# Attention: projection and row maxima in one block, four heads a unit, and q turned once

## The reference, cut to what matters

```python
qkv = x @ w_attn.T;  q, k, v = split(qkv, 3)      # 32 heads of 16
q, k = rope(q), rope(k)
scores = q @ k.T / 4;  scores[above the diagonal] = -inf
y = softmax(scores) @ v
ak, av = split(adapter_wte @ w_attn.T, 3)[1:]     # 10 rows
y = y + gating * softmax(q @ ak.T / sqrt(512)) @ av
out = y @ w_proj.T
```

## Time and profile before

| what | value |
|---|---|
| median of 3 runs | 2019.07 us (2018.42 to 2019.97) |
| the profiled execution's own time | 2018.18 us |
| its span | 2016.4 us |
| granted TensorE clock, mean | 0.954 of full |
| TensorE matmul, weight load busy | 1873.7 us (93%), 1486.5 us (74%) |
| VectorE, ScalarE, POOL busy | 1386.6, 1172.4, 1367.8 us |

### The profile page before, as it was taken

One profiled execution on the slowest core, in us unless ns is written; L12 is line 12 of the kernel. 1 busy time (PEld: TensorE's weight loads), 2 busy tenths in 40 slices (PEclk: granted clock), 3 DMA queues, 4 the chain that ended last, 5 costly groups with the idle time before them and its releaser, 6 DMA issues. The chain is left out here.

```text
span 2016.4 us, 32469 instructions
## 1 busy us (share of the span) xinstructions
PE 1873.7 (93%) x10700; PEld 1486.5 (74%) x10700; DVE 1386.6 (69%) x1799; ACT 1172.4 (58%) x2109; POOL 1367.8 (68%) x1349
## 2 busy tenths in 40 slices
PE   6989998766999999999999999999999999999967
PEld 4855776555788778777878787787788788877855
DVE  5547454567676787678778767876787687668756
ACT  3221333334776667576757766675767577667723
POOL 4000100352999799789969996997899699969844
PEclk9966899877999999999999999999999999999978
DMA  3000000103334233233333432332333334323301
GB/s 105 1 1 11 12 1 1 32 27 100 115 124 122 82 108 115 86 115 121 105 97 100 132 109 92 99 122 80 117 120 112 90 109 127 105 95 97 118 19 56
DMA packets 174859, 170.35 MB, mean 84 GB/s; under 512 B 11072, under 2 KB 142272, under 8 KB 174656
## 3 DMA queue, kind: packets, MB, share of 16 engines
q1 hardware_dynamic: 173696, 167.84, 27.2%
q10 hardware_dynamic: 960, 0.05, 0.0%
HBM read 165.22 MB, written 2.62 MB: 83 GB/s over the span
## 5 line engine op out<-in xcount | busy, mean ns | idle before, releaser
L143 PE MATMUL ps<-mix_xnT_hi,mix_w_hi 128*128 128x512 f32 x1152 | 463.8, 403 | 12.1 <-DVE mix_xT L1529 6.3
L145 PE MATMUL ps<-mix_xnT_hi,mix_w_lo 128*128 128x512 f32 x1152 | 455.9, 396 | 0.0
L144 PE MATMUL ps<-mix_xnT_lo,mix_w_hi 128*128 128x512 f32 x1152 | 455.5, 395 | 0.0
L1529 DVE SCALAR_TENSOR_TENSOR mix_xT<-ps,mix_cur,mix_xT 128x510 f32<-128x510 f32 x378 | 279.2, 745 | 140.1 <-ACT mix_xT L1396 131.2
L1347 POOL TENSOR_SCALAR_AFFINE_SELECT mix_spread<-mix_spread 128x256 f32<-128x256 f32 x512 | 308.1, 636 | 0.0
L1549 DVE TENSOR_TENSOR mix_decay<-mix_decay,mix_cb 128x1536 f32<-128x1536 f32 x128 | 302.7, 2402 | 4.5 <-ACT mix_decay L1422 4.5
L143 PEld LDWEIGHTS ps<-mix_xnT_hi,mix_w_hi 128*128 128x128 f32 x1152 | 217.9, 189 | 68.1 <-issue 12.5
L1445 ACT ACTIVATE mix_g_hi<-mix_gated 128x512 fp32r<-128x512 f32 x128 | 81.0, 633 | 318.2 <-POOL mix_gated L1324 286.2
L1420 ACT ACTIVATE mix_decay<-mix_spread,mix_cur_ncum 128x256 f32<-128x256 f32 x512 | 253.7, 495 | 13.2 <-DVE mix_cur_ncum L1601 13.2
L145 PEld LDWEIGHTS ps<-mix_xnT_hi,mix_w_lo 128*128 128x128 f32 x1152 | 217.6, 189 | 51.1
L144 PEld LDWEIGHTS ps<-mix_xnT_lo,mix_w_hi 128*128 128x128 f32 x1152 | 218.1, 189 | 47.3
(11 more groups left out here) (262 smaller groups left out, 3409.7 us busy)
## 6 DMA issues: line engine op xcount, KB each, us to landing
mix_spread<-cum_rows SPq DMA_DIRECT2D x128, 512.0 KB, 3.8
mix_w_raw<-in_w_in_stream SPq DMA_DIRECT2D x144, 256.0 KB, 4.9
mix_spread<-cum_rows SPq DMA_DIRECT2D x128, 256.0 KB, 4.8
mix_wo_raw<-in_w_out_T SPq DMA_DIRECT2D x64, 256.0 KB, 4.9
att_w_raw<-in_w_attn_T SPq DMA_DIRECT2D x12, 256.0 KB, 2.8
x<-in_x SPq DMA_DIRECT2D x8, 256.0 KB, 4.7
ffn_w_raw<-in_w_ffn_T SPq DMA_DIRECT2D x2, 1024.0 KB, 6.3
out_rows<-x SPq DMA_DIRECT2D x8, 256.0 KB, 2.0
```

Source lines behind the costliest of these rows:

```text
L143: pe.matmul(out, lh, rh, start=(k == 0), stop=False)
L144: pe.matmul(out, lh, rl, start=False, stop=False)
L145: last = pe.matmul(out, ll, rh, start=False, stop=(k == tiles - 1))
L1529: dve.scalar_tensor_tensor(out=d[:, :, shift:T], in0=src[:, :, 0:T - shift], scalar=w[:, MK - 1 - shift:MK - shift], in1=d[:, :, shift:T], ...
```

## The change

`setup` and its block are gone: SP loads one tile of x, four pieces of the weights (a ring of four), three tiles, and the rest between; POOL makes the constants at the head of the attention block and the masks behind the weights. VectorE makes two of the twelve low halves. POOL adds `rot` to the rows and clears v's padding. k is projected first, then q, then v. The products have banks 0 and 1, the scores 2 to 5, the turned layernorm 6, and turned k and q both 7. q is turned as it comes, into a `qT` for all rows. The row maxima are made in the same block, in 32 units of four heads on unrounded `qT` and `kT`. A unit writes its maxima into `qmax`, and stands between projections: batch 0 starts at tile 2, place 3, and so on, four places a tile; 7 units of batch 3 are left for the end. The softmax block no longer turns q: `m_turn` transposes a tile's `qmax` and adds it to all eight groups of `qT`. So each of a group's four heads has its maximum in row 16 + group of its slot, and k has its one there.

Cut to its core (the removed block is described above; the rope's products, the copy out of the adapter and renamings are left out):

```diff
-        at_least(pe, ln.s["lo"], t - 1)
+        at_least(pe, ln.s["lo"], t + 1 - banks)
         for k in range(KT):
-            last = pe.transpose(sh.ps[:, ln.bank0 + t % 2, k * P:(k + 1) * P],
+            last = pe.transpose(sh.ps[:, ln.bank0 + t % banks, k * P:(k + 1) * P],
                                 ln.xn[:, t % 2, k * P:(k + 1) * P], sh.ident[:, :])
...
+            COLUMN = (1, 0, 2)
             chunks = [(c, k) for c in range(3) for k in range(KT)]
+            BY_DVE = (1, 3)
...
+            def unit_slots():
+                return [(2 * b + 2, 3) for b in range(B)]
+            at_slot = {}
+            for b, (it, place) in enumerate(unit_slots()):
+                for hg in range(HG):
+                    at_slot[(it, place)] = HG * b + hg
+                    it, place = (it, place + 1) if place < 3 else (it + 1, 0)
+            ITERATIONS = NT + 1
...
+                load_x(0)
+                for n in range(NRAW):
+                    load_w(n)
+                for t in (1, 2, 3):
+                    load_x(t)
+                for n in range(NRAW, len(chunks)):
+                    load_w(n)
+                    if n % 2 and n // 2 + 2 < NT:
+                        load_x(n // 2 + 2)
+                for t in range(len(chunks) // 2 + 2, NT):
+                    load_x(t)
...
+                ln.rstd_pool(pool, 0)
+                lo_split(0)
+                ln.rstd_pool(pool, 1)
+                for n in range(2, len(chunks)):
+                    if n not in BY_DVE:
+                        lo_split(n)
+                    if n == 7:
+                        ln.rstd_pool(pool, 2)
+                pool.wait_ge(made, 4)
+                pool.affine_select(out=sh.mask_qk[:, :], in_=sh.zeros[:, :], compare_op=ALU.is_ge, fill=MASKED,
+                                   base=0, pattern=[[-1, P]], channel_multiplier=1).then_inc(made, 1)
+                pool.affine_select(out=sh.mask_kq[:, :], in_=sh.zeros[:, :], compare_op=ALU.is_ge, fill=MASKED,
+                                   base=0, pattern=[[1, P]], channel_multiplier=-1).then_inc(made, 1)
+                pool.tensor_copy(sh.ident16[:, :], sh.ident[:, :]).then_inc(made, 1)
+                pool.memset(av_bd[:, :, :, :], 0.0).then_inc(pool_padded, 1)
+                pool.memset(v[:, :, :, HD:SLOT], 0.0).then_inc(pool_padded, 1)
+                pool.wait_ge(pool_padded, 3)
+                pool.memset(v[:, :, :, HD:HD + 1], 1.0).then_inc(pool_padded, 1)
+                for t in range(NT):
+                    add_rot(t, 0)
+                    add_rot(t, 1)
+                    if t + 3 < NT:
...
-                        k_turn_out(t - 1)
+                        turn_to(qT, t - 1, 1, 0)
+                        turn_to(qT, t - 1, 1, 1)
+                    if t < NT:
+                        v_out(t)
+                        turn_to(kT, t, 0, 0)
+                        turn_to(kT, t, 0, 1)
...
+                def row_max(u):
+                    b, hg = units[u]
+                    dve.wait_ge(scored, u + 1)
+                    for qt, cols in ((0, slice(0, P)), (1, slice(P, BLK))):
+                        out = qmax[:, 2 * b + qt, :].rearrange("p (s r) -> p s r", r=SLOT)[:, :, HD + hg:HD + hg + 1]
+                        last = dve.tensor_reduce(out, ps[:, SCORE_BANK:SCORE_BANK + 4, cols], AX.X, ALU.max, negate=True)
+                    last.then_inc(maxed, 1)
...
+                    row_max_at(t, 0)
+                    if t < NT:
+                        rope(t, 0)
                     if t + 1 < NT:
                         ln.lo_dve(dve, t + 1)
+                    row_max_at(t, 1)
+                    if t < NT:
+                        rope(t, 1)
+                    row_max_at(t, 2)
+                    if t + 3 < NT:
+                        stats(t + 3)
+                    row_max_at(t, 3)
...
+                def turn(t, which, half):
+                    pe.wait_ge(rope_added, 2 * t + which + 1)
+                    at_least(pe, turn_out, 4 * t + 2 * which + half)
...
+                def scores(u):
+                    b, hg = units[u]
+                    if u == 0:
+                        pe.wait_ge(made, 7)
+                    if hg == 0:
+                        pe.wait_ge(turn_out, 4 * (2 * b + 2))
+                    at_least(pe, maxed, u)
+                    t0 = b * T
+                    for s in range(4):
+                        out, r = ps[:, SCORE_BANK + s, :], slice(32 * s, 32 * s + 32)
+                        pe.matmul(out[:, 0:P], qT[r, hg, t0:t0 + P], kT[r, hg, t0:t0 + P],
+                                  start=True, stop=False, skip_group_check=True)
+                        pe.matmul(out[:, P:BLK], qT[r, hg, t0 + P:t0 + T], kT[r, hg, t0:t0 + T],
+                                  start=False, stop=False, skip_group_check=True)
+                    for s in range(4):
+                        last = pe.matmul(diagonals(ps[:, SCORE_BANK + s, :]), sh.ident16[:, :],
+                                         sh.mask_qk[:, :].unsqueeze(1).broadcast_to([P, 2, P]),
+                                         start=False, stop=True, skip_group_check=True)
+                    last.then_inc(scored, 1)
...
+                    scores_at(t, 0)
+                    project(t, 0)
                     if t:
+                        turn(t - 1, 1, 0)
+                    scores_at(t, 1)
+                    project(t, 1)
+                    if t:
+                        turn(t - 1, 1, 1)
+                    scores_at(t, 2)
+                    project(t, 2)
+                    turn(t, 0, 0)
+                    scores_at(t, 3)
+                    turn(t, 0, 1)
...
+                scores_at(NT, 0)
+                turn(NT - 1, 1, 0)
                 pe.wait_ge(pre_done, 2)
+                pe.wait_ge(roped, 2 * NT)
+                adapter(2, 0)
+                scores_at(NT, 1)
+                turn(NT - 1, 1, 1)
+                pe.wait_ge(v_done, NT)
+                adapter(0, 1)
...
+                scores_at(NT, 3)
+                for u in range(HG * (B - 1) + 1, HG * B):
+                    scores(u)
...
-                if stage == "q_turn":
-                    for half in range(2):
-                        dve.tensor_copy(qT[:, (t // 2) % 2, 4 * half:4 * half + 4, (t % 2) * P:(t % 2 + 1) * P],
-                                        heads_of_bank(bank(n + half))).then_inc(aux_free, 1)
+                if stage == "m_turn":
+                    cols = qT[:, :, t * P:(t + 1) * P]
+                    dve.tensor_tensor(cols, cols, bank(n)[:, 0:P].unsqueeze(1).broadcast_to([P, HG, P]),
+                                      ALU.add).then_inc(aux_free, 1)
...
-                    if stage == "q_turn":
-                        last = turn_q(pe, t, part, out)
+                    if stage == "m_turn":
+                        last = pe.transpose(out[:, 0:P], qmax[:, t, :], sh.ident[:, :])
```

More of the change, by code:

```diff
@@ L146, in three_pass @@
     return last
[L149 to L173, removed]
 def build_attention(nc, sh, ins):
@@ new lines, in add_rot @@
+                def add_rot(t, which):
+                    pool.wait_ge(roped, 2 * t + which + 1)
+                    out = rows[:, which, t % 2, :, 0:HD]
+                    pool.tensor_tensor(out, out, rot[:, which, :, :], ALU.add).then_inc(rope_added, 1)
+                pool.memset(sh.mhalf[:, :], -0.5).then_inc(made, 1)
+                pool.memset(sh.ident[:, :], 0.0).then_inc(made, 1)
+                pool.memset(sh.zeros[:, :], 0.0).then_inc(made, 1)
+                pool.wait_ge(made, 3)
@@ L317, in _, with rope @@
             def _(dve):
-                def rope(t, which, out):
+                def rope(t, which):
                     n = 2 * t + which
-                    bank = (3 * t + which) % 4
+                    bank = (3 * t + which) % 2
                     src = ps[:, bank, :].rearrange("p (h d) -> p h d", d=HD)
+                    out = rows[:, which, t % 2, :, 0:HD]
                     co = cos[:, t % 2, :].unsqueeze(1).broadcast_to([P, HEADS, HD])
@@ new lines, in _ @@
+                dve.memset(rows[:, :, :, :, HD:SLOT], 0.0).then_inc(dve_padded, 1)
+                dve.wait_ge(dve_padded, 1)
+                k_slots = rows[:, 0, :, :, :].rearrange("p u (g s) r -> p u g s r", s=4)
+                for hg in range(HG):
+                    dve.memset(k_slots[:, :, hg, :, HD + hg:HD + hg + 1], 1.0).then_inc(dve_padded, 1)
+                stats(0)
+                stats(1)
+                for n in BY_DVE:
+                    lo_split(n)
+                ln.lo_dve(dve, 0)
@@ L355, in _ @@
+                stats(2)
+                dve.memset(qmax[:, :, :], 0.0).then_inc(dve_padded, 1)
+                dve.memset(a_bd[:, :, :], 0.0).then_inc(dve_padded, 1)
+                dve.wait_ge(dve_padded, HG + 3)
+                dve.wait_ge(misc, 16 * 4)
+                for t in range(ITERATIONS):
+                    row_max_at(t, 0)
```

(13 more changed lines are left out.)

293 lines of the change are left out of this document (114 added, 179 removed).

## The result

The changed kernel took 2011.52 us (median of 7 runs, 2010.69 to 2013.84), the kernel before 2019.07 (7 runs on the same chip, 2016.74 to 2019.97). The ratio is 0.9967 with a 95% interval of 0.9956 to 0.9978. It is faster, by 0.3%: 7.5 us by the medians, where 11.9 was forecast.

The account below looks back on a forecast made before the run. TensorE was taken as the limit in the projections and, at half clock, in the row-maximum block. Gains of 8.5 + 3.0 + 0.4 = 11.9 us off 2018.2 gave 2006.3, said as 2007; forecast 1999 to 2014 (chance 0.64), range 1994 to 2017.

Parts of the forecast that it names:

- The merged stage: Tiles 3 to 7, four units each between projections: 17.2 us a tile, 86 for five, ending at 141.0.
- more waits: Rival: another 2 us bare in each merged tile, five tiles give 10 back, about 2017 us; chance 0.11.
- of the clock: Rival: the clock falls to 1.2 GHz in the merged stage, costing 65 us, about 2072; chance 0.05.
- the fourfold price: Rival: unrounded products' four passes come on top of the rounded price, a unit 4.2 us, about 2102; chance 0.01.
- The start: Weights, constants and first rope additions, paced by POOL: first addition ends at 29.7 us, bounds 27 and 34.
- piece 4: A piece of weights at the start, its low half made by POOL; transferred, rounded and split at about 11 us.
- Tile 1: Projection tile with k and q both turned: 10.4 us plus 1.0 waiting on the single turn bank, 11.4.
- the last slots: After tile 7: two adapter products, two half turns, four units and two bare waits, 15.4 us, to 156.4.
- The tail: Units 25 to 31 alone: 3.4 us each at full clock, 4.6 at half; 32.5 in all, entry at 189.2.
- The softmax block's opening: Two transposes and two additions before the first score: 3.1 us instead of 6.1, gain 3.0.
- the six later turns: Later q turns in the softmax block become one transpose each, mostly under the exponential: gain 0.4 us in all.
- Everything behind attention is unchanged: Feed-forward, mixer and second feed-forward were forecast at their former times, 52.6, 1544.2 and 55.2 us.

Follow-up runs that it names:

- the repeat: The changed kernel measured once more with no edit: 2011.51 us, ratio 0.9972 to the kernel before.
- all three edits: Changed kernel with x's second tile loaded before the weights, v's padding cleared early on POOL, and two score bank sets for the last eight units: 1990.35 us.
- nothing merged: Changed kernel with all 32 units run behind the projections, none between them: 2085.07 us, one run.
- the twelve fillers: Twelve mask matmuls before the softmax block's first score: 2020.05 us on the changed kernel; 1995.22 with v's padding cleared early and two tail bank sets added.
- The fillers of the tail: Changed kernel with eight dummy 512-column matmuls between two tail units, into a free bank: 2007.65 us, ratio 0.9937.
- Eight fillers before the softmax block: Eight mask matmuls before the first score, on the changed kernel with v's padding cleared early and two tail bank sets: 1991.34 us.

## Why the prediction was right, and where it was off

The time lies in the range and on the side forecast, 4.5 us above the number. Point by point:

*The merged stage* was right. A tile takes 17.27 us (forecast 17.2), a unit 1.26 of TensorE (1.24), the bare wait 1.04 (1.3), the two reductions 1.82 together (1.8), and the clock is 1.00. With that the rivals of more waits, of the clock and of the fourfold price fall. The four heads' products take 0.9 us (87.67 to 88.56): eight in the kernel, 16 matmuls in the trace, so two for each unrounded product, where a rounded one has one. The rule of the Trainium skill (FP8 and Floating Point Precision, TensorE Precision Notes) that I weighed, four passes for true FP32, would have made a unit 4.2 us if the passes came on top of the rounded price; the trace says 1.26, so here they don't.

*The start* was the first term to fail. The step that failed is that piece 4 "is split at about 11", and with it "tile 0's second transpose batch ... at 31.7". POOL waited 3.86 us for tile 1's statistics, took 1.84 for its scalars, and came to piece 4 at 14.27; TensorE was through with the batch at 34.7, 3.0 late. The operations were sized rightly (memset 3.50 for 3.8, addition 1.29 for 1.28), and the eight pieces with the scalars took 11.9 us for 11.7. But tile 1 of x now stood behind those four pieces, and POOL serves in order. I had counted what is put into POOL's queue and not what SP's new order makes late. Tile 1 then took 13.0 us for 11.4, mostly because its first projection began at half clock (3.97 us, where tile 2's took 2.85), which I hadn't reckoned with. Tile 2 took its 11.9. With 0.3 us from tiles 3 to 7 and 0.2 in the last slots, the first of the last eight units starts at 160.29 instead of 155.2. (The terms that I named for the last slots add up to 14.7 and not to 15.4; the missing 0.7 are about the transposes at line 539, 0.66 us, which I didn't name.)

*The tail* was 2.5 us too short, 36.2 us from there for eight units where the forecast makes 33.7. Both prices of a unit were right; "one or two of seven still fast" was wrong, none is. The clock falls within the first of the eight units (line 490 takes 0.57 us, line 492 then 1.13 instead of 0.63), behind a bare wait of 1.42 us. The larger oversight was one of kind: I read the tail as a matter of latency and clock, and didn't ask which banks are free in it. Two sets there are worth 18.4 us of entry, twice what the merge was to gain there by my own count.

*The softmax block's opening* took 2.90 us for 3.1, and the six later turns gave 0.07 us each, 0.4 as said. 163.4 us is the forecast, and three executions without fillers in that block have it (the repeat, all three edits, nothing merged). The others lie from 161.8 to 170.6, by the stretches at half clock, which the forecast didn't treat; against the 166.8 of this execution of the kernel before, that is anything from a gain of 5 us to a loss of 4. In the profiled execution of the changed kernel a dip inside the block cost 1.6 us, the end 0.6, the sooner return of the clock at the start gave 1.0, and it took 164.4.

*"Everything behind attention is unchanged"* holds for the code and not for the time: 2.5 us came off there. The same mixer code took 1542.1 to 1545.0 us in these kernels, leaving out those with fillers ahead of the softmax block. The kernel before, with 1544.2, lies within that spread. Where in it a kernel falls was not explained, so I count these 2.5 us as no merit of the change: without them the profiled executions would be 3.2 apart, and that the time lies well inside the range owes something to luck.

So 11.9 forecast less 5.1 of the start and what follows it, less 2.5 of the tail, less 1.0 in the softmax block, plus 2.5 behind attention is 5.8, the 5.65 of the profiled executions. The medians of all runs have it at 7.5. The repeat's profiled execution, without the dip, has a span of 2009.6, 1.1 less; what else lies between the two figures is the spread of single executions.

## What to carry to other kernels

When transfers are reordered, write down for each in-order engine what it needs next and when that lands; the wait that was bought off here at the weights was found again behind the transfer that was put back. When producers run out and a chain of two engines is left alone, give it the buffers that the finished stage no longer needs before thinking of its clock (18.4 us of entry here, where fillers gave 4.4). And a change of a few instructions in one block has to be judged by the whole time, with each later stage cut out and compared, because it can cost more in code that it doesn't touch than it gains at home, as the twelve fillers did.

## What the runs showed that I had not expected

Twelve small matmuls shortened one block by 6.5 us and lengthened another, with the same code, by 10, through waits that no row explains. Two sets of banks brought the clock back by themselves (0.97 instead of 0.51). The fillers of the tail, the first of them at 167.90, had full clock from about 172 us on. Eight fillers before the softmax block didn't bring it back where twelve did. The Trainium skill says that "the default state is throttled, and activity releases the throttle" (TensorE: Matmul & The Clock Gate, Part 1: The HAM clock gate); the windows of the twelve agree, with 0.94 in place of 0.50; those of the eight show 0.50 up to 181 us, as without fillers.
